# A message-passing layer over 200,000 edges: tiles of 127 edges instead of 128, and gathers that name 127 rows

## The reference

```python
msg_in = jnp.concatenate([nodes[row], nodes[col], edge_features], axis=-1)
messages = _mlp(msg_in, mW1, mb1, mW2, mb2)          # relu(. @ W1 + b1) @ W2 + b2
aggregated = jax.ops.segment_sum(messages, col, num_segments=nodes.shape[0])
upd_in = jnp.concatenate([nodes, aggregated], axis=-1)
return _mlp(upd_in, uW1, ub1, uW2, ub2)
...
x = _layernorm(x + layer(x, src, dst, edge_attr_32, ...))
```

## Time and profile before

| | |
|---|---|
| three runs | 2620.52, 2624.29, 2624.53 us; median 2624.29 |
| profiled execution | span 2629.5 us from first to last instruction; no other time of it is given |
| span against the median | 5.2 us (0.2%) longer |
| TensorE busy | 2171.8 us, 83% of the span |
| GpSimd busy | 1500.2 us, 57% |
| VectorE, ScalarE busy | 785.5 and 787.3 us, 30% each |
| mean granted TensorE clock | 0.780 of full speed |
| moved by DMA | 89.82 MB, 34 GB/s |

### The profile page before, as it was taken

How to read it: one execution, slowest core, us unless ns; L and a number is a source line. 1 busy time by engine, 2 the same in 40 slices (tenths; PEclk the granted TensorE clock), 3 DMA queues, 4 the chain that set the end, 5 groups by cost and what they waited for, 6 DMA issues and landing times.

```text
span 2629.5 us, 44108 instructions
## 1 busy us (share of the span) xinstructions
PE 2171.8 (83%) x14372; PEld 1907.7 (73%) x14372; DVE 785.5 (30%) x2197; ACT 787.3 (30%) x2078; POOL 1500.2 (57%) x1572
## 2 busy tenths in 40 slices
PE   2988888888888788888888888888888888888897
PEld 2877777777768677777787767777677767777676
DVE  3222222222222222222222333333333333333334
ACT  3222222222222222222223333333333333333333
POOL 6655555555556555665555555555555555555550
PEclk9777677777776867787777788877877877787878
DMA  5111111111111111111111111111111111111110
GB/s 118 36 34 32 32 34 32 32 32 32 33 32 33 34 31 32 32 35 32 32 30 31 32 33 32 32 31 33 32 31 31 33 32 32 31 31 34 31 32 19
DMA packets 97107, 89.82 MB, mean 34 GB/s; under 512 B 58534, under 2 KB 58954, under 8 KB 96730
## 3 DMA queue, kind: packets, MB, share of 16 engines
q0 software_dynamic: 50016, 51.32, 11.0%
q1 hardware_dynamic: 33610, 30.90, 4.5%
q10 hardware_dynamic: 13458, 7.31, 1.3%
HBM read 86.20 MB, written 3.21 MB: 34 GB/s over the span
## 4 chain that ended last, share of the span: by engine, by line
PE 56%; another core or an unknown queue 20%; issue 14%; DVE 5%; ACT 3%; ACTq 1%; DVEq 1%; DMA 0%; SPq 0%
PE bank L280 13%; PE bank L281 13%; PE bank L291 11%; PE bank L266 5%; PE bank L256 5%; PE bank L295 3%; PE bank L253 3%; DVE oh_t L343 1%; PE bank L638 1%; PE bank L631 1%; ACT xe L310 1%; PE bank L625 1%; ACTq L364 1%; DVE xc L360 1%
## 5 line engine op out<-in xcount | busy, mean ns | idle before, releaser
L234 POOL DMA_INDIRECT xg<-x_rows,slot_idx x1563 | 1499.1, 959 | 1071.1 <-DVE slot_idx L349 636.9
L280 PE MATMUL bank<-w_xe,xe 97*128 97x128 f32 x3128 | 792.5, 340 | 58.7 <-issue 57.4
L281 PE MATMUL bank<-win_tab,oh_t 96*128 96x128 f32 x3128 | 768.0, 332 | 69.0 <-issue 67.7
L281 PEld LDWEIGHTS bank<-win_tab,oh_t 96*128 96x128 f32 x3128 | 622.7, 244 | 79.7 <-issue 78.8
L280 PEld LDWEIGHTS bank<-w_xe,xe 97*128 97x128 f32 x3128 | 620.9, 244 | 75.8 <-issue 75.3
L333 DVE TENSOR_TENSOR oh<-iota,rel 128x384 f32<-128x384 f32 x391 | 218.3, 559 | 1306.5 <-remote 980.0
L291 PE MATMUL bank<-oh,hid 128*128 128x96 f32 x3128 | 535.6, 321 | 55.6 <-issue 53.8
L310 ACT ACTIVATE xe<-bank 64x256 f32<-64x256 f32 x782 | 295.7, 378 | 897.2 <-remote 580.3
L291 PEld LDWEIGHTS bank<-oh,hid 128*128 128x128 f32 x3128 | 505.3, 241 | 74.2 <-issue 72.7
L325 ACT ACTIVATE hid<-bank 128x512 f32<-128x512 f32 x391 | 230.8, 590 | 785.2 <-remote 440.8
L343 DVE COPY oh_t<-bank 96x512 f32<-96x512 f32 x391 | 268.5, 687 | 474.7 <-remote 294.6
(11 more groups left out here) (58 smaller groups left out, 533.2 us busy)
## 6 DMA issues: line engine op xcount, KB each, us to landing
xe<-edge_t SPq DMA_DIRECT2D x391, 64.0 KB
xg<-x_rows,slot_idx POOLq DMA_INDIRECT x1563
xc<-x_t ACTq DMA_DIRECT2D x4, 800.0 KB
resid<-x_rows SPq DMA_DIRECT2D x24, 128.0 KB
out<-resid ACTq DMA_DIRECT2D x24, 128.0 KB
resid<-dst_groups SPq DMA_DIRECT2D x1, 784.0 KB
dst_i<-dst_tiles ACTq DMA_DIRECT2D x1, 784.0 KB
src_idx<-src_all SPq DMA_DIRECT2D x1, 784.0 KB
```

What stands on the lines that cost most here:

```text
L234: pool.indirect_dma_start(out=xg[:, k, j * D:(j + 1) * D], out_offset=None, in_=x_rows, in_offset=bass.IndirectOffsetOnAxis(ap=slot_idx[:, ...
L280: nc.tensor.matmul(o, xe[:, r, j * P:(j + 1) * P], w_xe[:, :], start=True, stop=False)
L281: last = nc.tensor.matmul(o, oh_t[:, q, j * P:(j + 1) * P], win_tab[:, r, :], start=False, stop=True)
```

## The change

A constant LANES = 127 becomes the number of edges in a tile. The tiles keep 128 partitions; the last one is padding (on the host: src 0, dst 12500, edge features 0). Tiles, groups and laps are counted from 127: 1575 tiles, 394 groups, 50 laps, UPD_LAP 27. Each gather names the first 127 entries of its column of indices and writes 127 partitions; the 32 gathers of lap 0 name all 128, so that partition 127 of every slot holds a row of x from then on. Two conditions are widened for a last lap that has two groups. No engine operation changes its shape.

```diff
+LANES = 127
 TPG = 4
 GE = TPG * P
 UNROLL = 8
-GROUPS = -(-N_EDGES // (GE * UNROLL)) * UNROLL
+GROUPS = -(-N_EDGES // (TPG * LANES * UNROLL)) * UNROLL
...
-G_END = -(-N_EDGES // GE)
-T_END = -(-N_EDGES // P)
+G_END = -(-N_EDGES // (TPG * LANES))
+T_END = -(-N_EDGES // LANES)
...
-        def gather(pool, g, k, tiles=TPG):
+        def gather(pool, g, k, lanes=LANES, tiles=TPG):
...
-                    out=xg[:, k, j * D:(j + 1) * D], out_offset=None, in_=x_rows,
-                    in_offset=bass.IndirectOffsetOnAxis(ap=slot_idx[:, c:c + 1], axis=0),
+                    out=xg[0:lanes, k, j * D:(j + 1) * D], out_offset=None, in_=x_rows,
+                    in_offset=bass.IndirectOffsetOnAxis(ap=slot_idx[0:lanes, c:c + 1], axis=0),
...
             for k in range(UNROLL):
-                gather(pool, k, k)
+                gather(pool, k, k, lanes=P)
...
-                    gather(pool, g, g % UNROLL, min(TPG, T_END - g * TPG))
+                    gather(pool, g, g % UNROLL, tiles=min(TPG, T_END - g * TPG))
...
-                    bases = window_bases(ET.Activation, first, min(UNROLL, G_END - first) if
+                    bases = window_bases(ET.Activation, first, max(1, min(UNROLL, G_END - first)) if
...
-                        if not (isinstance(g, int) and g < 2):
+                        if not (isinstance(g, int) and (g < 2 or g - 2 >= G_END)):
...
+    def by_lane(a, fill):
+        rows = np.full((TILES * LANES,) + a.shape[1:], fill, a.dtype)
+        rows[:N_EDGES] = a
+        lanes = np.full((TILES, P) + a.shape[1:], fill, a.dtype)
+        lanes[:, :LANES] = rows.reshape((TILES, LANES) + a.shape[1:])
+        return lanes.reshape((TILES * P,) + a.shape[1:])
```

More of the change, by code:

```diff
@@ L28 @@
 UNROLL = 8
-GROUPS = -(-N_EDGES // (GE * UNROLL)) * UNROLL
+GROUPS = -(-N_EDGES // (TPG * LANES * UNROLL)) * UNROLL
 ITERS = GROUPS // UNROLL
-EDGES = GROUPS * GE
 TILES = GROUPS * TPG
@@ L56 @@
 EPS = 1e-5
-assert EDGES == TILES * P and GROWS * GPP == GROUPS and CHUNKS % TAIL == 1
+assert LANES <= P and TILES == GROUPS * TPG and GROWS * GPP == GROUPS and CHUNKS % TAIL == 1
 assert (ITERS - 1) * UNROLL < G_END <= GROUPS and 2 * GPP == UNROLL and TSTEPS % TSLOTS == 0
@@ L1035 @@
     x, src, dst, edge = (np.asarray(a) for a in (x, src, dst, edge_attr_32))
-    pad = EDGES - N_EDGES
-    src_p = np.concatenate([src, np.zeros(pad, src.dtype)])
-    dst_p = np.concatenate([dst, np.full(pad, N_NODES, dst.dtype)])
-    edge_p = np.concatenate([edge, np.zeros((pad, DE), edge.dtype)])
+    def by_lane(a, fill):
[4 more added lines that the diff above has]
+        return lanes.reshape((TILES * P,) + a.shape[1:])
+    src_p, dst_p, edge_p = by_lane(src, 0), by_lane(dst, N_NODES), by_lane(edge, 0)
     x_p = np.concatenate([x, np.zeros((NODES - N_NODES, D), x.dtype)])
```

## The result

The changed kernel takes 4480.98 us (median of three, 4479.8 to 4482.14) against 2624.29: ratio 1.707, 95% interval 1.7025 to 1.7115. The profiled execution took 4479.8 us with a span of 4478.1. The forecast was 2661, the range ended at 2766.

A forecast was written before the change was run, and what follows sets the result against it. TensorE was taken as the bound, with GpSimd's gathers hidden. One more looped lap (+52.3 us) less 15.1 us from a shorter last lap gave +37.2 us, so 2661 us on the 2624.3 median; range 2624 to 2766.

The forecast's parts named there:

- the gathers' issue price: GpSimd's time to issue a 127-row gather: 0.93 us taken, hidden, against 944 ns for 128 rows; upper bound doubled.
- The threshold: GpSimd's gather spacing: a looped lap of 32 gathers allows 1.63 us each before issue counts, 0.38 us free.
- Rival C: GpSimd's issue becomes the bound because an odd count costs more; at double, about 3450 us; chance 0.07.
- Rival D: Every gather's transfer uses the same one DMA engine, 2.96 us each, some 4650 us in all; chance 0.05.
- The landing: Gather transfers: on one engine they would land some 2.8 us later, within the room before their readers, so 0.
- The tiles: Three more groups from 127-edge tiles: one looped lap more, +52.3 us, less 15.1 from a shorter last lap, +37.2 us.
- the naive count: Three added groups at 6.54 us each: +19.6 us, 2644 us in all, which the prediction called too low.
- looped laps: TensorE's laps of eight groups: 52 to 53 us without an update chunk, 53 to 54 with one.
- the last lap and its bare chain: Last lap cut to two groups: 8.6 us of work saves 21.4 us; chunk 22's uncovered steps take 7.0 us, net +6.3.
- Rivals A and B: One-engine gathers disturb TensorE less (A, 2556 us at a tenth) or more (B, 2714 to 2766); chance 0.06 each.

The follow-up runs named there:

- e6: Kernel before, with only the first of a group's four gathers naming 127 rows after the first lap, the others 128: 2625.55 us beside 2628.43.
- e7: Kernel before, with one gather a group of 127 stand-in rows of 1024 bytes in place of four: 1636.42 us beside 2628.43.
- e2: Kernel before (128-edge tiles, 391 groups), with all gathers after the first lap naming 127 rows: 4441.69 us beside 1993.92.
- e10: Changed kernel with all gathers naming 128 rows, run again at the upper level: 2655.96 us beside the kernel before's 2625.79, ratio 1.0126.
- e1: Changed kernel (127-edge tiles) with all gathers naming 128 rows, at the lower level: 2016.41 us beside the kernel before's 1993.92, ratio 1.0114.
- e8: Kernel before, with one gather a group of 128 stand-in rows of 1024 bytes in place of four: 1633.26 us beside 2628.43.
- e3: Kernel before, with gathers of 121 rows after the first lap: 2092.44 us beside 1993.92.
- e13: Kernel before, with GpSimd's lead in the looped laps cut from 8 groups to 3, at the lower level: 2002.03 us beside 1989.82, ratio 1.0061.
- e9: Kernel before, unchanged, run again for a profile: 2626.81 us.
- e11: Kernel before, with gathers of 64 rows after the first lap: 2653.81 us beside 2625.79.
- e17: Kernel before, with GpSimd's lead in the looped laps cut from 8 groups to 3, at the upper level: 2643.71 us beside 2626.89, ratio 1.0068.
- e5: Kernel before, with gathers of 127 rows after the first lap, each row 128 bytes instead of 256: 4437.8 us beside 2628.43.
- e12: Kernel before, with gathers of 124 rows after the first lap: 2529.29 us beside 2625.79.

## Why the prediction was wrong

**The step that failed** is the gathers' issue price. It said: "Lower bound: a hundred-and-twenty-eighth less, 0.93 us, hidden. Upper bound: doubled", and took the lower. Measured: 2.54 us, 2.7 times, beyond both bounds. The threshold beside it, a gather every 1.63 us before it counts, was about right at the level it was made for: one every 1.66 us in the mean (e6) left the time as it was, and at 2.85 us every gather counts in full. But it is not free slack below a need of TensorE's: with one every 1.59 us (124 rows) GpSimd was already the bound, and the kernel was faster. At the lower level there is none: 121 rows, at 1.01 us a gather, cost 4.9%.

**Rival C** was the mechanism: GpSimd the bound. Its own price was too small (1.88 us, about 3450 us in all), its chance (0.07) too. The reason given against it, "7 ns a row in the row at hand leaves little to grow", divided by the wrong number: the cost goes by rows per engine, 8 for 128 rows and 127 for 127. With the rule on how a count is dealt in hand, the prediction used it for the landing alone and never asked what the one who deals pays. It could not have read the 13.4 ns from one row count, but it could have let the upper bound go with the share, 16 times, instead of doubling.

**Rival D** named 4567 us of gathers and 4650 in all, near the 4481 measured, by a mechanism that is refuted (e7): right number, wrong reason, a matter of luck. In e2 the packets with a gather's rows take some 2.1 us of one engine, not 2.96, and would have fitted into the 2.85 us between gathers even on one engine.

**The landing**, "0 either way": right. It never became the bound: GpSimd's gathers (3956.4 us) and the steps between them (459.8 and 20.4) fill all but some 40 us of the span, so TensorE's 1596.6 us of waiting for gathers are waiting for their issue.

**The tiles**, +37.2 us: measured apart (e10) +30, interval 26 to 40, and the naive count of +19.6 lies below. Most parts hold within 1 us of the forecast: looped laps of 52.1 us without and 53.0 with a chunk in e10, from branch to branch of TensorE, the last lap and its bare chain as above. One was missed. The sum has "the groups that go are the cheap ones", as if the price belonged to the last lap; in e10 the groups behind the last gather are as cheap, and five of them now lie in the last looped lap, which took 44 us instead of 53. With that the sum is 37.2 - 9 = +28, and the interval admits both. At the lower level, where GpSimd binds, it is +22 (e1): 12 gathers at 1.25 us are 15, and the bare chain would be the rest.

**Rivals A and B**, that gathers disturb TensorE: at the upper level there is a coupling, and it is far larger than a tenth. With one gather a group TensorE needs 1633 us (e8). The argument against it, that the quiet last lap is also straight code, falls with e10, whose looped code was as quick once the gathers had ended. That it is the number of gathers and not the rows is supported by 64 rows with 279 stops beside e8 without one, in two batches of the same level; the mechanism is not shown.

## What to carry to other kernels

Name a number of rows that 16 divides in an indirect gather; here GpSimd's price for one was set by rows / k with k the largest divisor up to 16, 0.84 us plus 13.4 ns for each, and one row fewer than 128 nearly triples it. When an operand's size changes, price the engine that issues the transfer as well as the transfer, and let the upper bound follow how the work is dealt. Fewer and wider gathers are worth more here than any of it, if the data can be laid out for it: some 1634 us with one or two a group where four took 1990 to 2626, in runs that fetched stand-in rows and did not compute the layer.

## What the runs showed of the hardware

- DMA engines that get no row of a gather still get as many 4-byte elements as the others get rows: 15 x 127 x 4 bytes a gather in e2.
- Single-engine gathers go to changing engines: 391 of them, 5.9 us of one engine each, hid behind 4.2 us a group (e7).
- The kernel before runs at about 1992 or about 2626 us, by batch, with the same program. At the upper level TensorE stops inside runs of matmuls (231 and 291 gaps above 0.5 us) and the granted clock is 0.78. At the lower one there are no such gaps in any profile (e1, e3, e13 and others), the clock of the kernel before is 0.98 to 1.00, and with 128 rows GpSimd is the bound at 1.25 us a gather (e1). Within batches at the upper level the stops were there when GpSimd made four gathers a group and got ahead (e9, e10, e11, e17), and not when GpSimd was the bound (e5, e6, e12) or made one gather a group (e7, e8). They gather where gathers follow each other without a pause for more than four, and beside one row of 31 TensorE took 38 us for a group (e17). Yet at the lower level 1543 gathers in a row, 1.25 us apart, brought none (e1). What causes them, and why they come by batch, stays open. Not run at the upper level: 16 rows, two gathers a group, and gathers spaced out with full rows.
